# The second product of a split: y @ Wo with its four wo_hi passes first and its wo_lo passes on 64 rows, in pairs

## The reference

```python
def L0(x, conv_w, conv_b, Wp, bp, Ws, bs, A_log, dt_log, Wo, bo):
    conv = conv_b + sum(x_pad[:, k:k+L, :] * conv_w[k, 0] for k in range(K))   # K = 128
    proj = conv @ Wp + bp
    B_t, C_t = softplus(proj[..., :N]), tanh(proj[..., N:])
    u = x @ Ws + bs
    decay = 1.0 + dt * A
    # over L: state = decay * state + dt * B_t * u ; y = C_t * state
    return y @ Wo + bo                                # y: (B, L, 64), Wo: (64, 512)

def L1(x, h0, Wx, Wh, b):
    # over L: h = tanh(h @ Wh + x_t @ Wx + b)
    return hs

x = x + L0(x, cond[:, None, :], ...)
x = x + L1(x, cond, Wx, Wh, b)
```

## Time and profile before

| | us |
|---|---|
| median of 3 runs | 1181.25 (1179.35 to 1182.19) |
| the profiled execution | 1180.59 |
| its span, first to last instruction | 1178.7 |
| PE busy (matmul) | 1149.1 |
| DVE busy | 717.1 |
| ACT busy | 556.3 |
| GpSimd busy | 364.0 |

### The profile page before, as it was taken

The page is one execution under the profiler, slowest core; times in us unless marked ns, Lnnn a source line. Parts: engine busy times, 40 slices in busy tenths (PEclk is TensorE's granted clock), DMA queues, the critical chain, the costliest instruction groups (busy, mean ns, idle before and its releaser), DMA issues.

```text
span 1178.7 us, 16600 instructions
## 1 busy us (share of the span) xinstructions
PE 1149.1 (97%) x5984; PEld 953.7 (81%) x5984; DVE 717.1 (61%) x1158; ACT 556.3 (47%) x815; POOL 364.0 (31%) x210
## 2 busy tenths in 40 slices
PE   6999999988999999999999999999999999999997
PEld 6889898965788888888888888888888888888886
DVE  5786868776655555556555565555555655556553
ACT  2574737454345445453545454544545354545431
POOL 1000504134133333333333333333333333333330
PEclk9999999999999999999999999999999999999999
DMA  9719092631122222222222222222222222222202
GB/s 357 294 55 378 3 340 94 217 132 36 37 72 72 72 82 94 87 92 72 71 71 71 71 71 71 71 71 82 94 85 94 72 71 71 71 71 72 72 36 72
DMA packets 56899, 121.35 MB, mean 103 GB/s; under 512 B 3936, under 2 KB 7008, under 8 KB 56864
## 3 DMA queue, kind: packets, MB, share of 16 engines
q1 hardware_dynamic: 56864, 120.87, 30.3%
HBM read 87.30 MB, written 33.55 MB: 103 GB/s over the span
## 4 chain that ended last, share of the span: by engine, by line
PE 95%; DVE 2%; issue 1%; DMA 0%; ACT 0%; POOL 0%; SPq 0%; POOLq 0%; DVEq 0%; ACTq 0%
PE bank L813 10%; PE bank L731 10%; PE bank L821 10%; PE bank L822 10%; PE bank L807 10%; PE bank L825 10%; PE bank L806 10%; PE bank L875 5%; PE bank L753 3%; PE bank L780 3%; PE bank L786 3%; PE bank L796 2%; PE bank L797 2%; PE bank L761 2%; PE bank L762 2%; PE bank L763 2%
## 5 line engine op out<-in xcount | busy, mean ns | idle before, releaser
L349 POOL TENSOR_TENSOR x_lo<-x_f,x_hi 128x512 fp32r<-128x512 f32 x124 | 156.6, 1293 | 555.9 <-ACT x_hi L451 555.9
L483 ACT ACTIVATE h_f<-z_f 128x512 f32<-128x512 f32 x128 | 80.9, 632 | 295.0 <-DVE z_f L679 295.0
L689 DVE TENSOR_TENSOR hT_lo<-bank,hT_hi 128x512 fp32r<-128x512 f32 x128 | 88.6, 692 | 187.7 <-ACT hT_hi L487 187.7
L821 PE MATMUL bank<-wh_hi,hT_hi 128*128 128x512 f32 x512 | 200.4, 391 | 0.0
L822 PE MATMUL bank<-wh_lo,hT_hi 128*128 128x512 f32 x512 | 199.9, 390 | 0.0
L807 PE MATMUL bank<-wx_lo,x_hi 128*128 128x512 f32 x512 | 199.6, 390 | 0.0
L806 PE MATMUL bank<-wx_hi,x_hi 128*128 128x512 f32 x512 | 199.2, 389 | 0.0
L679 DVE TENSOR_TENSOR z_f<-bank,b_rows 128x512 f32<-128x512 f32 x128 | 88.6, 692 | 130.0 <-PE bank L825 129.3
L343 POOL TENSOR_TENSOR x_lo<-x_f,x_hi 128x2048 fp32r<-128x2048 f32 x32 | 147.7, 4615 | 18.3 <-ACT x_hi L456 18.3
L813 PE MATMUL bank<-wx_hi,x_lo 128*128 128x512 f32 x512 | 144.8, 404 | 0.3 <-POOL x_lo L349 0.3
L825 PE MATMUL bank<-wh_hi,hT_lo 128*128 128x512 f32 x512 | 137.1, 389 | 0.0
(11 more groups left out here) (89 smaller groups left out, 1631.6 us busy)
## 6 DMA issues: line engine op xcount, KB each, us to landing
x_ring<-x_rev SPq DMA_DIRECT2D x64, 512.0 KB, 7.6
x_f<-x_dtb SPq DMA_DIRECT2D x32, 1024.0 KB, 8.4
out<-x_f SPq DMA_DIRECT2D x31, 1024.0 KB, 5.3
t_ring<-bands SPq DMA_DIRECT2D x64, 256.0 KB, 6.7
w_f<-Wx SPq DMA_DIRECT2D x1, 1024.0 KB, 5.4
w_f<-Wh SPq DMA_DIRECT2D x1, 1024.0 KB, 5.1
out<-x_f SPq DMA_DIRECT2D x4, 256.0 KB, 2.3
turned<-Wp SPq DMA_DIRECT2D x3, 128.5 KB, 3.0
```

What stands on the lines that cost most here:

```text
L349: nc.gpsimd.tensor_tensor(x1_lo[:, c], x1_f[:, par, c], f(x1_hi[:, c]), ALU.subtract)\
L689: nc.vector.tensor_tensor(hT_lo[:], turned_h, f(hT_hi[:]), ALU.subtract).then_inc(htlo_ready, 1)
L821: nc.tensor.matmul(z, hT_hi[:, k], wh_hi[:, k], start=start and k == 0, stop=False)
```

## The change

wo_product first issues the four wo_hi passes, one for each chunk, on all 128 rows. Then it issues the four wo_lo passes on 64 rows each, with y_hi alone, so that Wo_lo*y_lo is no longer part of the result. Chunks 0 and 2 read both operands from partitions 64 to 127 (y_hl's y_hi), chunks 1 and 3 from partitions 0 to 63, where a new tile y_h2 holds a copy of y_hi. The new copy is made by ACT (y_copy_low), in step s = 2 between hT_hi and x1_copy. PE has a new wait for it ahead of the first wo_lo pass.

```diff
+        y_h2 = sb(ctx, "y_h2", [N, G * BATCH], F32R)
...
+            def y_copy_low(g):
+                act.wait_ge(yhi_ready, g + 1)
+                nc.scalar.copy(y_h2[:], y_hl[N:P, :]).then_inc(yh2_ready, 1)
...
                 if m == 30:
                     y_copy(0)
+            y_copy_low(0)
             split_x_chunk(2)
...
                     if s == 2:
+                        y_copy_low(g + 1)
                         x1_copy(g + 1, 1 - par)
...
                     nc.tensor.matmul(XB[c][:], wo_hi[:, bass.ts(c, P)], y_hl[:], start=True, stop=False)
-                    nc.tensor.matmul(XB[c][:], wo_lo[:, bass.ts(c, P)], y_hl[:], start=False, stop=True)\
+                pe.wait_ge(yh2_ready, g + 1)
+                for c in range(KC):
+                    rows, y_high = (slice(0, N), y_h2[:]) if c % 2 else (slice(N, P), y_hl[N:P, :])
+                    nc.tensor.matmul(XB[c][:], wo_lo[rows, bass.ts(c, P)], y_high, start=False, stop=True)\
                       .then_inc(wo_done, 1)
```

More of the change, by code:

```diff
@@ L180, in build @@
         yhi_ready = sem("yhi_ready")
+        yh2_ready = sem("yh2_ready")
         ylo_ready = sem("ylo_ready")
```

## The result

| | before | after |
|---|---|---|
| median of the runs, us | 1181.72 (1179.35 to 1182.41, 4 runs) | 1199.78 (1198.82 to 1201.16, 4 runs) |
| profiled execution, us | 1180.59 | 1199.47 |
| its span, us | 1178.7 | 1197.7 |

The ratio is 1.0157, with a 95% interval of 1.0139 to 1.0175: 1.6% slower, at 1199.8 us where 1199 was forecast.

A forecast was written before the change was run, and what follows sets the result against it. PE was full, but GpSimd's x1_lo would hold it: 30 x 0.38 + 0.68 + 0.80 = 12.9 us, plus 32 x 0.16 = 5.1 for d, +18.0 on 1180.59; 1199 us forecast for the median, range 1192 to 1207.

The forecast's parts named there:

- PE has no hole and a pass is worth 0.227 us: PE in the recurrence: busy practically throughout; truly paired passes turn eight pitches into six, saving 0.454 us a group.
- wo_done comes three pitches and d later: First chunk of y @ Wo: its last pass starts 0.68 us later by the order, plus d.
- d: On PE before the first 64-row wo_lo pass: cost of the shape change, 0 to 0.35 us, taken as 0.16.
- The slack of 0.30 us: Between GpSimd's x1_lo and PE's use of it: 1.39 less 1.09 us, leaving PE 0.38 us late a group.
- The sign that I named for d: In the profile after: distance from the fourth wo_hi pass to the first wo_lo pass, less 0.23 us.
- The reading by which the load comes only after a full drain: At the shape change on PE: weight load strictly after drain, d 0.27 to 0.35 us, time 1203 to 1205.
- Way back and pairs cost nothing: On PE: return to 128 rows and unoverlapped pairs are free up to 0.83 us together; their bounds add to 0.80.
- the hold: Ahead of step 3's L813: PE waits for GpSimd's x1_lo, until 0.38 us plus d later.
- The saving at step 3 is given back on DVE: DVE's z_f begins as before or up to 0.1 us earlier, so the transposes stand where they stood despite 0.454 saved.
- First and last group: The two end groups: the first pays 0.80 us plus d, the last, without slack, 0.68 us plus d.
- The copy y_h2 is covered: ACT's copy, 0.62 us, ends about 0.2 us before PE wants its first wo_lo load: cost 0.

The follow-up runs named there:

- the order alone: Kernel before with only the order changed: four wo_hi passes, then four wo_lo passes, all on 128 rows, no copy; 1193.61 us, ratio 1.0109.
- The three doses: Kernel before, all passes on 128 rows, with two, three or four wo_hi passes ahead of the first wo_lo pass: 1181.50, 1187.42, 1193.61 us.
- unpaired: Changed kernel with its four 64-row wo_lo passes one after the other on rows 64 to 127, without y_h2, copy or wait: 1200.09 us.
- the kernel with both holds gone: Changed kernel with x1_lo's fourth chunk made by DVE instead of GpSimd, and DVE's step 2 addition of h moved behind step 3's z_f: 1181.10 us.
- the changed kernel without GpSimd's hold: Changed kernel with the fourth chunk of x1_lo made by DVE in step 3 instead of by GpSimd: 1181.13 us, ratio 1.0000.

## Why the prediction was right

- **PE has no hole and a pass is worth 0.227 us.** So it is: pairs overlap fully and save 0.444 a group where PE decides.
- **wo_done comes three pitches and d later.** 0.88 us, of which 0.68 is the order: with the order alone it was 0.68 to the hundredth.
- **The slack of 0.30 us behind it, read from one waiting group against an ordinary one.** The three doses show it. This step carried the forecast: two thirds of the loss.
- **d.** I took 0.16 between 0 and 0.35; it is 0.20. That adds 32 x 0.04 = 1.3 us. The size was near, the make-up was wrong: I had the pass in flight leaving, 0.16, and the load hidden. Measured, the first wo_lo pass starts 1.01 us after the first wo_hi pass where 4 x 0.227 = 0.91 is in pitch, so the wait is 0.10; and the load, which starts with its pass, is bare, so that the pass lasts 0.50 instead of 0.39, which is 0.11. One part was 0.06 too long and the other was missing with 0.11; that they nearly cancel is luck. The sign that I named for d, where the first wo_lo pass starts, shows the 0.10 alone; the 0.20 is seen at DVE's start. The reading by which the load comes only after a full drain, 0.27 to 0.35, was too much.
- **Way back and pairs cost nothing, being inside the hold.** Right: unpaired is 27.948, paired 27.946. The way back is 0.21, inside its bounds.
- **The saving at step 3 is given back on DVE.** This step was wrong in its reason. It also moved DVE by 0.68 alone and left d out, by which z_f does come late: 634.79 - 629.94 = 4.85 us after the first wo_hi pass, where it was 627.46 - 622.72 = 4.74. That lateness of 0.1 us is taken up by the load's lead. What gives the saving back is PE itself, by the two changes of shape; the outcome at that place, the transposes where they stood to 0.1 us, is the same, and that is luck. The sum did not depend on the reason, since GpSimd held PE behind it; but had DVE been the one that gives the saving back, the kernel with both holds gone would have come out at 1167, and it took 1181.10.
- **First and last group.** The last paid 0.88 (0.68 + 0.20), as worked out. The first paid 0.7 and not 1.0: its L788 stands at 305.65, 8.50 us after the product's first pass at 297.15, against 304.80 - 297.01 = 7.79. DVE's four sums ran in 2.73 us there instead of 2.93, having no further waits among them, which is 0.2 of the 0.3; the sums also began 0.1 earlier than worked out.
- **The copy y_h2 is covered.** It ends at 629.68 + 0.61 = 630.29, 0.33 us before the load would have come in pitch, at 630.62.

Together: 30 x 0.576 = 17.3, and 1.6 for the two ends, are 18.9 of the 19.0 us by which the span grew. Forecast were 18.0: d adds 1.3, the first group takes 0.3 away.

## What to carry to other kernels

A full engine says nothing of how close the others are behind it. Before an accumulation is reordered on it, look up who waits for the first finished piece, follow that chain to where it comes back, and read the slack there; a group that already waits for it shows the latency to subtract. And passes saved on PE by another shape have to pay for two changes of shape, 0.41 us here, which is the pitch of 1.8 passes: the two saved here in one stretch bought nothing that could be measured, so it takes more than two.

## What the runs showed of the hardware

**A change between 128-row and 64-row passes costs 0.20 to 0.21 us each way**, and half passes on different halves of the rows start within 0.01 us of each other (both at 630.95, both at 631.29).

**DVE's subtraction with both inputs in SBUF stretches beside GpSimd.** Chunk four of x1_lo on DVE took 1.82 us (median of 31). The same instruction in the first group, with GpSimd idle, takes 0.68 (median of the four, which take 2.49 together). DVE and GpSimd in the changed kernel without GpSimd's hold:

```profile
628.39 1.83 DVE L690 TENSOR_TENSOR x_lo<-x_f,x_hi 128x512 fp32r<-128x512 f32 x1
...
627.12 2.55 POOL L351 TENSOR_TENSOR x_lo<-x_f,x_hi 128x512 fp32r<-128x512 f32 x2
629.62 5.07 POOL L345 TENSOR_TENSOR x_lo<-x_f,x_hi 128x2048 fp32r<-128x2048 f32 x1
```

With both holds gone:

```profile
630.16 1.51 DVE L696 TENSOR_TENSOR x_lo<-x_f,x_hi 128x512 fp32r<-128x512 f32 x1
...
627.32 3.80 POOL L351 TENSOR_TENSOR x_lo<-x_f,x_hi 128x512 fp32r<-128x512 f32 x3 [18.54 <-ACT x_hi L457]
```

DVE's first row starts 1.28 us before GpSimd's third chunk ends (628.39 and 629.67) and ends 0.55 after it (630.22), as if it had run only then. The second starts 0.96 before that end (630.16 and 631.12), takes 0.32 less, and again ends 0.55 after it (631.67). GpSimd's next instruction takes 5.07 instead of 4.61 (medians). The Trainium skill's page SBUF — State Buffer, section SBUF: two separate sides, says that the two engines lock one pair of ports against each other for a whole instruction, on DVE for instructions with two SBUF inputs among others. These rows agree with it. No run here took the contention away by itself, and it cost nothing that could be measured (27.352 us a group), since DVE had two idle microseconds there.
